# Splitting the row maxima on another engine, and moving slices of side work, in a fused attention and expert layer

## The reference, cut to what matters

```
x = x + layernorm(attn(layernorm(x)))          # 16 heads of 16, rope, causal window of 250
x = x + layernorm(ffn(layernorm(x)))

ffn(src):  q = src@Wq; k = src@Wk_c@Wk; v = src@Wv_c@Wv; rope
           sa = softmax(q k' / 4) v @ Wo        # 16 heads, every key seen
           x  = rmsnorm(src + sa)
           shared = swiglu(x@W_shared_in) @ W_shared_out
           h = swiglu(x@W1_shared)
           routed = sum over 8 experts of (h @ W2[e]) * w[:, e]   # top 2 of a group
           out = rmsnorm(x + shared + routed)
```

## Time and profile before

| | |
|---|---|
| Three runs | 2000.43 us median (1998.41 to 2009.91) |
| Profiled execution | 1989.7 us, of it 1987.9 us span |
| PE busy | 1838.3 us (92%) |
| DVE busy | 1359.4 us (68%) |
| ACT busy | 807.2 us (41%) |
| POOL busy | 378.3 us (19%) |
| Mean granted TensorE clock | 0.959; at 9 tenths or more in all of the last 36 of 40 slices |

### The profile page before, as it was taken

The page is one execution under the profiler, slowest core; times in us unless marked ns, Lnnn a source line. Parts: engine busy times, 40 slices in busy tenths (PEclk is TensorE's granted clock), DMA queues, the critical chain, the costliest instruction groups (busy, mean ns, idle before and its releaser), DMA issues.

```text
span 1987.9 us, 27962 instructions
## 1 busy us (share of the span) xinstructions
PE 1838.3 (92%) x9216; PEld 1026.2 (52%) x9216; DVE 1359.4 (68%) x4206; ACT 807.2 (41%) x1730; POOL 378.3 (19%) x669
## 2 busy tenths in 40 slices
PE   6868899999999999999999999999999999999987
PEld 4343363735556364654637455463645536374456
DVE  6447475685768668685786857687586857868467
ACT  3433535335342544335353353525433363533510
POOL 1337014101241012300141002410123101420010
PEclk8566999999999999999999999999999999999999
DMA  3016002201022100311022010220103111130420
GB/s 109 2 64 244 33 22 87 85 2 54 23 101 82 40 16 23 138 44 44 33 79 104 2 54 23 97 86 10 45 23 138 44 44 33 51 121 2 181 85 11
DMA packets 31297, 123.05 MB, mean 62 GB/s; under 512 B 5425, under 2 KB 18353, under 8 KB 26545
## 3 DMA queue, kind: packets, MB, share of 16 engines
q1 hardware_dynamic: 28624, 105.54, 14.8%
q0 software_dynamic: 2528, 15.73, 2.1%
HBM read 101.33 MB, written 18.87 MB: 60 GB/s over the span
## 4 chain that ended last, share of the span: by engine, by line
PE 73%; DVE 17%; issue 5%; ACT 3%; DMA 1%; SPq 0%; POOL 0%; DVEq 0%; ACTq 0%; POOLq 0%
PE fb L847 12%; PE ot L786 10%; PE sm L745 8%; PE fb L825 6%; DVE negmax L1210 6%; PE st L772 5%; PE fb L821 4%; PE st L713 3%; PE dn L713 3%; PE fb L843 3%; PE st L729 3%; DVE sm L1207 2%; DVE acc L1408 2%; PE sm L772 2%; PE ot L713 2%
## 5 line engine op out<-in xcount | busy, mean ns | idle before, releaser
L625 ACT ACTIVATE probs<-st 128x512 f32<-128x512 f32 (+3 forms) x832 | 395.4, 508 | 387.8 <-PE st L772 383.9
L847 PE MATMUL fb<-w_r,h_r 128*128 128x512 f32 x1344 | 393.0, 419 | 0.0
L745 PE MATMUL sm<-k_t,q_t 48*128 48x512 f32 (+3 forms) x864 | 314.1, 449 | 64.7 <-DVE negmax L1207 32.1
L1210 DVE TENSOR_REDUCE negmax<-sm 128x1 f32<-128x512 f32 x416 | 268.8, 685 | 86.7 <-PE sm L745 86.5
L772 PE MATMUL st<-q_t,k_t 64*128 64x512 f32 (+3 forms) x832 | 298.9, 453 | 22.6 <-ACT probs L625 19.9
L745 PEld LDWEIGHTS sm<-k_t,q_t 48*128 48x128 f32 x864 | 144.2, 195 | 313.9 <-DVE negmax L1207 139.4
L847 PEld LDWEIGHTS fb<-w_r,h_r 128*128 128x128 f32 x1344 | 231.7, 189 | 93.0 <-issue 57.0
L1207 DVE CUSTOM_DVE_ANT_0 sm<-sm,mask_qk 128x384 f32<-128x384 f32 (+1 forms) x448 | 202.6, 469 | 88.6 <-PE sm L745 85.4
L786 PE MATMUL ot<-probs,v_s 128*32 128x512 f32 (+3 forms) x2048 | 252.7, 536 | 2.3 <-POOL probs L500 2.3
L459 POOL TENSOR_TENSOR stack<-rot,stack 128x256 fp32r<-128x256 f32 x64 | 50.0, 782 | 994.7 <-ACT stack L561 994.7
L772 PEld LDWEIGHTS st<-q_t,k_t 64*128 64x128 f32 x832 | 133.5, 193 | 122.7 <-ACT probs L625 87.9
(11 more groups left out here) (213 smaller groups left out, 2614.7 us busy)
## 6 DMA issues: line engine op xcount, KB each, us to landing
w_r<-w_parts SPq DMA_DIRECT2D x30, 2048.0 KB, 7.9
wup_r<-wup_parts SPq DMA_DIRECT2D x32, 512.0 KB, 4.1
w_parts<-w_r POOLq DMA_DIRECT2D x4, 2048.0 KB, 9.4
x_s<-in_L_attn_query SPq DMA_DIRECT2D x8, 512.0 KB, 4.7
q_t<-rot_b SPq DMA_DIRECT2D x256, 4.0 KB
x_kept<-o_s SPq DMA_DIRECT2D x8, 512.0 KB, 3.0
h_s<-in_L_ffn_W_experts POOLq DMA_DIRECT2D x8, 512.0 KB, 5.3
xa<-x_kept SPq DMA_DIRECT2D x8, 512.0 KB, 3.3
```

Of the source, the lines that this page charges most:

```text
L625: nc.scalar.activation(probs[:, n % PSLOTS, 0:hi - lo], score_bank(m)[:, 0:hi - lo], ACT.Exp, scale=float(D) ** -0.5).then_inc(s_ex, 1)
L745: mm(max_bank(w, a)[:, 0:hi - lo], q_t[r:r + MROW, b, t * P:(t + 1) * P], k_t[r:r + MROW, b, lo:hi], start=True, stop=True).then_inc(s_sm, 1)
L847: last = mm(fb[q % 2][:, :], h_r[:, h, m, rows], w2_r[:, k % 2, w, m, :], start=(m == 0 and n == 0), stop=(m == NH - 1 and n == 2))
L1210: return v.tensor_reduce(negmax[:, g % 2, n // GH, c:c + 1], max_bank(g * UNITS + n, a)[:, 0:hi - lo], AX.X, ALU.max, negate=True).then_in ...
```

## The change

Three things change, in the seven passes with side work.

1. The split of the maxima moves from DVE to POOL (`split_max` in the list of POOL, the same two operations on the same data). In the first half group 0 is split ahead of the masks, and groups 1 to 3 after the mask of the score units 2 and 3 of groups 0 to 2. In the second half the four splits stand in a row. DVE gets a wait on the split before it overwrites `negmax`, two groups later.
2. In the second half the slices of `QUIET_OUT` that stood at step 2 of groups 1 to 3 stand at step 3, as in group 0, and the fifteen slices of the lead end at step 0, not at step 1.
3. In place of the two unread products stands the first slice of tile 7. The other three stay in `heads`.

```diff
-QUIET_OUT = [g * UNITS + n for g in range(NGR) for n in ((2, 8, 12) if g else (3, 8, 12))]
+QUIET_OUT = [g * UNITS + n for g in range(NGR) for n in (3, 8, 12)]
...
-OUT_HEADS = {0: ((), (), slices(18, 0, 2), slices(18, 2, 3), slices(18, 3)), 1: ((), slices(7), (), slices(8, 0, 2), slices(8, 2))}
-OUT_AT = [-LEAD] + spread(len(OUT_BESIDE) * NH - len(QUIET_OUT) - 1, 1 - LEAD, 1) + QUIET_OUT
+OUT_HEADS = {0: ((), (), slices(18, 0, 2), slices(18, 2, 3), slices(18, 3)), 1: ((), slices(7, 1), (), slices(8, 0, 2), slices(8, 2))}
+OUT_AT = [-LEAD] + spread(len(OUT_BESIDE) * NH - len(QUIET_OUT) - 1, 1 - LEAD, 0) + QUIET_OUT
...
+            def split_max(i, a, gr):
+
+                count = (i - 1) * N_MS + a * NGR + gr + 1
+                pool.wait_ge(s_mx, i * N_MX + (a * NGR + gr + 1) * UNITS)
+                if gr >= 2:
+                    pool.wait_ge(s_mp, i * N_MP + a * NGR + gr - 1)
+                m = negmax[:, gr % 2].rearrange("p t (b h) -> p h b t", b=2)
+                hi = m_split[:, gr % 2, :, 0]
+                lo = m_split[:, gr % 2, :, 1]
+                g.tensor_copy(hi, m).then_inc(s_mh, 1)
+                pool.wait_ge(s_mh, count)
+                g.tensor_tensor(lo, m, hi.bitcast(F32), ALU.subtract).then_inc(s_ms, 1)
...
                     last.then_inc(s_mk, 1)
+                    if f is not None and m % UNITS == 2 and m // UNITS + 1 < NGR:
+                        split_max(i, 0, m // UNITS + 1)
...
                 rows_low(i - 1, i * N_SP + 16)
+                split_max(i, 0, 0)
                 mask_probs(i, i - 1)
                 low_parts(i, 1)
+                for gr in range(NGR):
+                    split_max(i, 1, gr)
...
                 if f is not None:
-                    unread(st[1], 2)
+                    expert_out(f, 7, 0)
...
-                        take_max(i, a, *divmod(m + LEAD, UNITS))
+                        gr, n = divmod(m + LEAD, UNITS)
+                        if f is not None and gr >= 2 and n == 0:
+
+                            dve.wait_ge(s_ms, i * N_MS + a * NGR + gr - 1)
+                        take_max(i, a, gr, n)
...
-                    if (m + LEAD) % UNITS == UNITS - 1 and m + LEAD < ALL:
+                    if f is None and (m + LEAD) % UNITS == UNITS - 1 and m + LEAD < ALL:
                         split_max(i, a, (m + LEAD) // UNITS)
```

More of the change, by code:

```diff
@@ L226, in build @@
         s_ms, N_MS = sem("max_split"), 2 * NGR
+        s_mh = sem("max_high_made_by_pool")
         s_mp, N_MP = sem("max_transposed"), 2 * NGR
```

## The result

The changed kernel takes 1982.95 us (median of 15 runs) and the kernel before, on the same chip, 2004.24 us: a ratio of 0.9916 [0.9893, 0.9940]. One run of each kernel stood far out (3811.74 us before, 2427.44 after) and is left out of the ratio, which is why it isn't the quotient of the two medians. In the bound that the prediction named this is "no change", which it gave 0.90. The profiled execution takes 1981.7 us, of it 1979.9 span; before it took 1989.7.

The account below looks back on a forecast made before the run. The chain of waits was 73% PE's own work and 17% DVE's. The terms -5.9 - 5.4 + 10.2 = -1.1 us, against the median of 2000.43 us, gave 1999 us, range 1986 to 2010.

Parts of the forecast that it names:

- no change: Outcome within about 1%, 20 us, of the kernel before, the least a measurement can tell; chance 0.90.
- Part 1: Split moved from DVE to POOL: saves time in second half's groups 0 and 1, -0.84 us per pass, -5.9 in all.
- POOL's split fits: POOL's pair, some 0.65 us with handovers, fits the 0.93 us before PE's transposes (first half, group 0), costing nothing.
- PE waits for POOL's split: Rival: in the first half a 1.76 us pair on POOL delays four transposes by 0.83 us each, +23 us; chance 0.08.
- Part 2: First slice of tile 7 replaces the unread products in `heads`: PE and DVE 0.77 us earlier per pass, -5.4 us.
- DVE is what the following lead is bound by: Step after `heads`: DVE bounds the second half's lead, so going on 0.77 us earlier counts in every pass.
- Part 3: Second half's slices from step 2 to 3: groups 1, 2, 3 cost +0.53, +0.53, +0.4 us per pass, +10.2 us.
- The sum of the order: All terms of the forecast for the seven passes with side work together: -1.1 us.
- a sentence on the lead's end: Second half's lead ending at step 0, not 1: counted as nothing, between -0.2 and +0.2 us per pass.
- its low end: Lower limit of the predicted range for the whole kernel: 1986 us.
- the wait at step 6: Sign in group 0, second half: PE's wait for DVE becomes about 1.0 us, not 1.43.

Follow-up runs that it names:

- experiment 1: Kernel before with only the split moved from DVE to POOL; slices and unread products as before: 1989.0 us, ratio 0.9965.
- experiment 4: Kernel before with the split on POOL and the first slice of tile 7 for the unread products, other slices at their old steps: 1985.09 us, ratio 0.9935.
- experiment 9: Kernel before with only the end of the lead's slices moved from step 1 to step 0: 1995.73 us, ratio 1.0005.
- the 81 runs: Runs of the kernel before, unedited, beside the experiments: mean granted clock 0.9528, average time 1997.4 us.
- Part 3 alone: Kernel before with only the quiet slices at step 3 in groups 1 to 3 and the lead's end at step 0: 2006.82 us, ratio 1.0041.
- the repetition: The changed kernel measured again with no edit, against the kernel before: 1982.04 us, ratio 0.9935.
- experiment 8: Kernel before with the split on POOL, the first slice of tile 7 and the lead's end at step 0; quiet steps unchanged: 1976.69 us, ratio 0.9918.
- experiment 6: Kernel before with four unread products of 256 columns in the second half's lead: 2005.96 us, ratio 1.0051.
- experiment 11: Kernel before with unread products lightly filling the second half's lead and PE's wait at step 6 of group 0: 1993.06 us, ratio 0.9982.

## Why the prediction was right and wrong

- **Part 1 (forecast -5.9 us)** was right: -0.84 us by step 16, and -0.76 for the whole second half when done alone. The reason was right too: only the two splits on which PE waits count.
- **POOL's split fits**: right. In the pass shown PE pauses for it by 0.15 us in the first half and 0.07 in the second, in all about 1.4 us over the program, where nothing was expected and 0.3 at once was the sign of being wrong. (The sum for the pair, two of 0.25 and two handovers of 0.1 us, makes 0.70 and not 0.65; measured were 0.51.) So the rival "PE waits for POOL's split" did not happen at the size that it named.
- **Part 2 (-5.4)** had the mechanism and twice the size: -0.38 us per pass, or -2.7. The third rotation came 0.72 us earlier; 0.33 us of it went where the earlier rotation met POOL's subtraction (56 passes without and 42 with Part 2 show it). The step "DVE is what the following lead is bound by" did not ask what DVE itself would run into.
- **Part 3 (+10.2)** had the mechanism and a size 1.6 times too large: 0.44 + 0.36 + 0.09 = 0.89 us per pass, +6.2. Two readings failed: the transposes ahead of a slice last 0.42 us, not 0.58, in each of the three groups, and in group 3 the slice covers ACT almost entirely: from the outputs to the next `weigh` it is 2.00 us, and 1.89 before.
- **The sum of the order** was -1.1 us and is -2.3. Two errors, of 2.7 and 4.0 us, pulled in opposite directions and mostly cancelled: that the sum came out near is luck in part.
- **What failed is a sentence on the lead's end**: "where DVE is the bound the order is indifferent. I count nothing". For the order that holds (107.66 and 107.63 us). For the clock it is the larger part of the effect. With the split off DVE and the last slice a step earlier, PE's pause of 0.27 us near the end of the lead disappears; neither does it alone (experiments 1, 4 and 9). Among the 14 traces of the table the seven with that pause have 16 dips at 41 to 43 us in 49 passes, the seven without it none in 49.
- The prediction took the clock as given. It read 0.959 and nines in every slice and never asked what lies in the missing hundredths; the three runs shown spread over 11.5 us, which by 1.35 us for each 0.001 is a spread of 0.0085 in the clock, within what the 81 runs show (0.942 to 0.961). So it had no rival "the pauses that the change closes hold the clock", and its low end, made of the order and the spread, was too high.
- It also expected the wait at step 6 at 1.0 us. That is what Parts 1 and 2 give (1.01); in the changed kernel it is 0.47 and 0.28, again because of the lead's end.

What stays open: why a given pause brings the clock down in one pass and not in the next; the two dips at 48 to 49 us of Part 3 alone, where no wait was longer than 0.53 us; the dips in first halves; and some 5 us of the first comparison, whose 0.9916 goes beyond the 0.994 of order and clock (the repetition gave 0.9935). There the runs of the kernel before averaged 2001.7 us, against 1997.4 for the 81 beside the experiments, and their clocks are not on record. Of the kernels run, experiment 8 has the shortest order, 0.87 us per pass below the changed kernel, and a median 5.4 us below it on the same chip; the two ratios overlap, so the times alone don't settle it. By the order Part 3's step 3 in groups 1 to 3 should be taken back, and its other half kept.

## What to carry to other kernels

A stage in which PE waits a little and often for another engine has two prices, the waits and the clock. Before costing an edit at nothing because its engine is not the bound, look at the granted clock in windows of a few us and at the pauses ahead of each fall. When several parts are put together, try each number of each part alone: here one that moves no time by order kept the clock up together with Part 1, and the other half of the same part cost 6 us.

## What the runs showed of the hardware

- The granted clock fell to 1.2 GHz behind pauses of PE of 0.1 to 0.3 us that followed each other (experiment 4: 0.27 us and less), and behind single ones of 1.4 us (experiment 6), for 3.4 us up to some 14, at 1.4 us and more a time. The Trainium skill ("TensorE: Matmul & The Clock Gate", HAM oscillation) tells of a kernel that lost the clock at every wait for a transfer. These traces agree that waits bring it down, but here they are waits on VectorE and much shorter, and they do it only in some passes: the 0.27 us pause in 16 of 49.
- Work that nobody reads can pay for itself: experiment 11 issues 84 instructions of PE more than the kernel before and is not slower (0.9982 [0.9959, 1.0005]); in experiment 6 too much of it made the kernel slower (1.0051).
- VectorE's addition with two SBUF inputs (128x512) took 0.99 to 1.06 us beside GpSimd's subtractions in the passes with side work, and 0.69 wherever GpSimd was idle (45 of 45 in the trace before).
- Four transposes of 128x128 took 0.37 to 0.42 us of PE's time ahead of a slice (512 columns, 128 rows), and 0.58 ahead of a unit (512 columns, 48 or 64 rows).
